# Turning the last stage's weights ahead of time, through DRAM, instead of inside the last stage

## The reference

```
def _L1_ffn_ref(x, gate_wq, gate_scale, up_wq, up_scale, down_wq, down_scale):
    def _dequant_linear(x, wq, scale):
        w = wq.astype(jnp.float32) * scale[:, None]
        return jnp.einsum('bsh,oh->bso', x, w)
    gate = _dequant_linear(x, gate_wq, gate_scale)     # gate_wq, up_wq: 1792 x 512
    up = _dequant_linear(x, up_wq, up_scale)
    h = jax.nn.silu(gate) * up
    return _dequant_linear(h, down_wq, down_scale)     # down_wq: 512 x 1792
...
h = _layernorm(x, axis=-1) * (1 + ca) + sa
x = x + ga * _L1_attn_ref(h, w_q, w_k, w_v, w_o)
h = _layernorm(x, axis=-1) * (1 + cb) + sb
x = x + gb * _L1_ffn_ref(h, gate_wq, gate_scale, up_wq, up_scale, down_wq, down_scale)
```

## Time and profile before

| | us |
|---|---|
| median of the runs | 1921.21 (1914.83 to 1922.13) |
| profiled execution, its own time | 1919.16 |
| its span | 1917.2 |
| PE busy | 1840.1 (96%) |
| PE weight loads busy | 1532.2 (80%) |
| DVE busy | 1265.4 (66%) |
| ACT busy | 1108.3 (58%) |
| POOL busy | 473.6 (25%) |
| HBM | 182.04 MB read, 109.05 MB written |

### The profile page before, as it was taken

One profiled execution on the slowest core, in us unless ns is written; L12 is line 12 of the kernel. 1 busy time (PEld: TensorE's weight loads), 2 busy tenths in 40 slices (PEclk: granted clock), 3 DMA queues, 4 the chain that ended last, 5 costly groups with the idle time before them and its releaser, 6 DMA issues. The chain is left out here.

```text
span 1917.2 us, 30131 instructions
## 1 busy us (share of the span) xinstructions
PE 1840.1 (96%) x9099; PEld 1532.2 (80%) x9099; DVE 1265.4 (66%) x3000; ACT 1108.3 (58%) x2581; POOL 473.6 (25%) x472
## 2 busy tenths in 40 slices
PE   6888889999999999999999999999999989999999
PEld 4456668888888888888888888888888867888887
DVE  5588867667677767666666766677676676544534
ACT  5564656667566656666666666666566654433423
POOL 3123242323424131232423123131312131010010
PEclk8898999999999999999999999999999999999999
DMA  9101365565655656576755646556564575111010
GB/s 355 70 1 66 121 193 174 183 211 158 207 175 180 191 157 184 147 226 202 220 173 160 191 141 187 164 163 186 155 186 145 155 236 166 61 50 66 5 60 22
DMA packets 193420, 292.09 MB, mean 152 GB/s; under 512 B 21304, under 2 KB 130872, under 8 KB 193344
## 3 DMA queue, kind: packets, MB, share of 16 engines
q1 hardware_dynamic: 192816, 290.11, 49.6%
q10 hardware_dynamic: 528, 1.05, 0.2%
HBM read 182.04 MB, written 109.05 MB: 152 GB/s over the span
## 5 line engine op out<-in xcount | busy, mean ns | idle before, releaser
L1777 PE MATMUL ps<-hA,wq 128*128 128x512 f32 x1536 | 387.2, 401 | 4.2 <-DVE qT L2253 4.2
L1843 PE MATMUL ps<-wo,oT 128*128 128x512 f32 x1536 | 367.7, 390 | 3.6 <-issue 2.1
L2096 ACT ACTIVATE pt<-pd 128x1280 fp32r<-128x1280 f32 x128 | 163.2, 1275 | 348.6 <-PE ps L1825 308.8
L2278 DVE CUSTOM_DVE_ANT_0 ps<-ps,mask 128x512 f32<-128x512 f32 (+3 forms) x512 | 235.9, 523 | 192.0 <-PE ps L1810 191.8
L1843 PEld LDWEIGHTS ps<-wo,oT 128*128 128x128 f32 x1536 | 287.6, 188 | 65.2 <-issue 5.1
L1777 PEld LDWEIGHTS ps<-hA,wq 128*128 128x128 f32 x1536 | 279.8, 189 | 61.2 <-issue 4.7
L2077 ACT ACTIVATE probs<-ps,nmax 128x512 f32<-128x512 f32 (+3 forms) x512 | 262.7, 532 | 96.5 <-DVE nmax L2278 96.3
L1825 PE MATMUL ps<-pt,V 128*128 128x512 f32 (+2 forms) x1152 | 255.5, 351 | 19.8 <-DVE pt L2302 19.4
L2085 ACT ACTIVATE probs<-probs,rinv 128x512 f32<-128x512 f32 (+3 forms) x512 | 246.3, 552 | 40.6 <-DVE rinv L2284 40.6
L1825 PEld LDWEIGHTS ps<-pt,V 128*128 128x128 f32 x1152 | 198.2, 192 | 49.0 <-issue 23.5
L1810 PE MATMUL ps<-kT,qT 128*128 128x512 f32 (+2 forms) x1152 | 225.3, 340 | 0.0
(11 more groups left out here) (236 smaller groups left out, 2612.9 us busy)
## 6 DMA issues: line engine op xcount, KB each, us to landing
turned_blocks<-tp SPq DMA_DIRECT2D x128, 640.0 KB, 3.0
pd<-turned_blocks SPq DMA_DIRECT2D x512, 160.0 KB, 3.3
wq_next<-in_L_attn_w_q_dram SPq DMA_DIRECT2D x16, 1024.0 KB, 7.0
wo_in<-in_L_attn_w_o_dram SPq DMA_DIRECT2D x16, 1024.0 KB, 7.2
wm<-in_L_wmod_dram SPq DMA_DIRECT2D x6, 2048.0 KB, 13.4
turned_values<-tv SPq DMA_DIRECT2D x32, 256.0 KB, 3.6
X<-in_L_attn_x_dram SPq DMA_DIRECT2D x4, 1024.0 KB, 11.1
wk_in<-in_L_attn_w_k_dram SPq DMA_DIRECT2D x16, 256.0 KB, 3.2
```

The source lines that it names most:

```text
L1777: last = nc.tensor.matmul(ps[:, bank, :], w[i][:, c, cols], hT[k][:, c, b * S:(b + 1) * S], start=(c == 0 and n == 0), stop=(c == DC - 1 a ...
L1843: last = nc.tensor.matmul(ps[:, bank, :], oT[x_][:, b, h, r * P:(r + 1) * P], wo[y_][:, h, :], start=(h == 0 and n == 0), stop=(h == GQ - ...
L2096: nc.scalar.activation(flat(pt[0][:]), flat(pd[:, u % 2]), ACT.Copy).then_inc(phi_done, 1)
L2278: nc.vector.tensor_tensor_reduce(out=v, in0=v, in1=mask[:, TB * P - KEYS[i]:], scale=-1.0, scalar=3e38, op0=ALU.add, op1=ALU.min, accum_ou ...
```

## The change

The 42 tiles of weights are cast and turned in attention's second half, groups 8 to 14, six tiles a group (two values of j), in units 1, 2, 3, 5, 6 and 7. For a tile, SP loads the int32 weights into `xr` one unit ahead (`load_tile`), ACT casts them to float in place, DVE turns the 32 x 32 blocks from `xr` into `hf_chunk` (`turn_tile`: two instructions of 256 columns for gate and up, one of 512 for down), and SP stores the four quadrants of partitions into a new DRAM tensor `turned_weights` (`store_tile`, four DMAs). Gate and up tiles are written in runs of 64 elements (256 B), down tiles in runs of 128 (512 B). `xr` and `hf_chunk` served the chunks of the second pair in groups 1 to 4 and are free later.

In the last stage the weights of a step j, gate, up and down together (768 KB), come back by four DMAs straight into the place where they are kept (`load_turned`). From j = 4 on a load waits for the gate product of step j - 4. The casts, PE's transposes, DVE's copies, the tensor `wb` and the identity in bf16 are gone. The elements of a kept gate or up tile lie in another order now, so PE reads the 128 columns of a block with a step of two elements (`weight`), and a down tile as runs of 32 elements (`down_weight`).

```diff
-                return [sb(late, f"gw{j}", [P, DC, P], F32R), sb(late, f"uw{j}", [P, DC, P], F32R),
-                        sb(late, f"dw{j}", [P, D], F32R)]
+                return sb(late, f"w{j}", [P, 3, D], F32R)
...
-                    body(NKV, False)
+                    body(NKV, False, True)
                     with eng.Fori(NKV + 1, NG - 1) as g:
-                        body(g, False)
+                        body(g, False, True)
...
+                TILE_UNITS = (1, 2, 3, 5, 6, 7)
+                turned_w = nc.dram_tensor("turned_weights", [FC, QD, 3, NQD, D], F32, kind="Internal").ap()
+                turned_v = turned_w.rearrange("(m e) j k b (a x) -> e k a m j b x", e=2, a=NQD)
+                turned_halves = turned_w.rearrange("(m e) j k b (h a x) -> e k a m j (b h) x", e=2, h=2, a=NQD)
...
+                def weight(j, k, c):
+                    return kept_weight(j, k).rearrange("p (h f e) -> p h e f", h=2, e=2)[:, c // 2, c % 2]
+
+                def down_weight(j):
+                    return kept_weight(j, 2).rearrange("p (a o i) -> p o a i", a=NQD, o=DC)
...
+                        def store_tile(g, i):
+                            m, e, k = steps_of(g), i % 2, i // 2
+                            sp.wait_ge(s["w_turned"], tile_no(g, i))
+                            for a_ in range(NQD):
+                                src = hf_chunk[QD * a_:QD * (a_ + 1), :]
...
+                                sp.dma_start(dst, src).then_inc(s["w_kept"], 16)
+
+                        def load_turned(j):
+                            if j >= 4:
+
+                                sp.wait_ge(s["gate"], j - 3)
+                            for b_ in range(NQD):
+                                rows_ = slice(QD * b_, QD * (b_ + 1))
+                                if j < FC - 1:
+                                    sp.dma_start(ww[j][rows_].bitcast(F32), turned_w[j, :, :, b_]).then_inc(ld_w[j % 4], 16)
...
+                                if keeps:
+                                    if u in TILE_UNITS:
+                                        store_tile(g, TILE_UNITS.index(u))
+                                    if u + 1 in TILE_UNITS:
+                                        load_tile(g, TILE_UNITS.index(u + 1))
+                                if not more and u == 6:
+                                    load_turned(1)
+                                if not more and u == 7:
+                                    load_turned(2)
+                                    load_turned(3)
+
+                                    sp.wait_ge(wo_split, GQ * NG)
+                                    load_turned(0)
...
                             if first:
-                                pe.wait_ge(s["prepped"], 3 * j + 3)
+                                pe.wait_ge(*loads_of(j))
...
-                            if j + AHEAD < FC:
-                                for q in range(3 * (j + AHEAD), 3 * (j + AHEAD) + 3):
-                                    turn_weights(q)
...
+                                if keeps and u in TILE_UNITS:
+                                    act.wait_ge(ld_w[0], 16 * tile_no(g, TILE_UNITS.index(u)))
+                                    nc.scalar.activation(xr[:], xr[:].bitcast(I32), ACT.Copy).then_inc(s["w_cast"], 1)
...
+                                if keeps and u in TILE_UNITS:
+                                    turn_tile(g, TILE_UNITS.index(u))
...
+                        def turn_tile(g, i):
+
+                            dve.wait_ge(s["w_cast"], tile_no(g, i))
+                            if not (at_group(g, NKV) and i == 0):
+                                dve.sem_inc(waits_seen, 1)
+                                dve.wait_ge(s["w_kept"], 16 * NQD * (tile_no(g, i) - 1))
+                            if i // 2 < 2:
+                                for h in range(2):
+                                    last = nc.vector.transpose(
+                                        out=hf_chunk[:].rearrange("p (b h i e) -> p h e b i", b=NQD, h=2, e=2)[:, h],
+                                        in_=xr[:, 2 * h:2 * h + 2, :].rearrange("p c (b j) -> p c b j", b=NQD))
```

More of the change, by code:

```diff
@@ L1507, in body @@
                                     sp.dma_start(at_first[:], att_t[0]).then_inc(ld_at_first, 16)
-                                if not more and u >= 6:
-                                    for q in range(2 * (u - 6), 2 * (u - 6) + 2):
-                                        load_weights(sp.dma_start, q)
                                 reached(sp, o_full, UNITS * g + (u - 1))
@@ L1953, in down @@
                                 for k in range(2):
-                                    last = nc.tensor.matmul(ps[:, t, :], hd[j][k][:, t * P:(t + 1) * P], ww[j][2][:],
+                                    last = nc.tensor.matmul(out, hd[j][k][:, t * P:(t + 1) * P], down_weight(j),
                                                             start=(j == 0 and k == 0), stop=(j == FC - 1 and k == 1))
```

224 lines of the change are left out of this document (82 added, 142 removed).

## The result

| | before | after |
|---|---|---|
| median, measured side by side | 1914.11 us (1911.41 to 1922.77, 20 runs) | 1920.33 us (1913.07 to 1932.79, 20 runs) |
| profiled execution, its span | 1917.2 | 1922.9 |

The ratio is 1.0033, 95% interval 1.0017 to 1.0049: the changed kernel is slower by 6.2 us, with 3.3 to 9.4 inside the interval. Forecast was 1909.

What follows compares the result with a forecast made beforehand. TensorE (PE) was taken as the bound, busy for all 530 us of attention's second half. 1919.2 - 16 (last stage) + 5 (attention) = 1908.2, or 1910.2 from the median of the runs shown; stated as 1909, range 1902 to 1914.

Steps and rivals of the forecast that it cites:

- Two access patterns change: Last stage: reading down weights in runs of 32 and gate and up weights with step two costs 0.
- The outer bound, +134: Last stage, strided gate and up loads: at twice 188 ns, each of 896 matmuls takes 376 instead of 226.
- Group 8, taken at 3 with bounds 1 to 8: Attention group at 885 to 970 us: its queue is already full, so the tiles cost PE 3 us.
- The last stage, -16, bounds 14 to 17.5: Last stage: removing transposes and casts saves 10.6 + 2.0 + 1.7 + 1.1 + 0.9 = 16.3 us, taken as 16.
- I cost the loads at 0: Last stage: 14 loads of 768 KB arrive in time; first weights there near 1568, first pair about 1573; cost 0.
- a wait of PE for it as a sign of being wrong: First batch of the last stage: PE waiting on the turned weights would show the prediction wrong.
- Groups 9 to 14, taken at 0.3 each: Attention, unit 6 to 7: tile lands late, PE waits 0.3 us per group; six groups 2 us, bounds 0 and 18.
- A: Attention's queue is tighter: packets near 83 ns, 3.0 us in six groups and 8 in the first, +26, 1929; chance 0.21.
- B: DMA engines bound the seven attention groups: 2001 at 165 ns a packet, 1935 to 1940 at about 120; chance 0.14.
- C: Last stage: the strided weight load costs from 227 ns on; twice 188 gives 2042; chance 0.06.
- D: Gain eaten in the flush: only the nine even sets of transposes count, 9 us, giving 1915; chance 0.04.
- The chance of 0.55: Whole kernel: probability given to the forecast, range 1902 to 1914, and to faster by about 0.5%, 9.6 us.

Runs made afterwards that it cites:

- e1_contig: Changed kernel with int32 tile rows loaded in another order and stepped DVE transposes, so TensorE reads all kept weights contiguously: 1916.73 us, ratio to before 1.0000.
- e3_psum_runs: Changed kernel with gate, up and down weights read contiguously and the down product written into PSUM in runs of 32: 1915.37 us, ratio to before 0.9994.

## Why the prediction failed, step by step

With three traces of each, the changed part adds up to: the last stage's gain, 178.2 - 165.4 = 12.8 up to the first down product; group 8, +8.7; the pace behind the first down product, +7.4; group 9, +0.1. Net +3.4. Forecast was -11, and the 14.4 between them are: the reads 8.9 (taken at 0), group 8 5.7 (8.7 for 3), the last stage 1.7 (14.3 for 16, at the old pace of the pairs), less 1.9 in the other groups (0.1 for 2). The ratio says +6.2, with 3.3 at its lower end; the 2.8 between are not traced to a row, and lie within what the stretch ahead of group 8 moves by.

- **"Two access patterns change", both taken at 0: this is the step that failed.** Measured 7.4 + 14 pairs x 0.11 = 8.9 us (9.1 by e1_contig against the changed kernel). The argument was that up to 226 ns of load nothing shows. The load record did stay under that, at 193 ns, and the matmuls came 233 apart all the same; with loads of 309 they came 235 apart. The rule compared the wrong two numbers: the pace did not follow the load's length on either side of 226. For the down weights I argued from the outputs product, and read it wrongly: its result is written into PSUM in runs of 32, but its moving operand `pt` is read in runs of 128, 96 or 64 elements. The access patterns in the trace of before say so ([128,4] with a median of 227 ns from matmul to matmul, against [32,4,4] and 233 for the down product after). Only the writing of short runs had been priced, and e3_psum_runs shows that it is indeed free. The outer bound, +134, was so far off that it hid how dear 3% of 1344 matmuls already is.
- The Trainium skill, "SBUF — State Buffer", section "Door 1: The DMA port swizzle", gave 0 for a step of two fp32 elements, since each 16-byte line is hit twice. The runs disagree: 233 ns for 226.6 on the stationary operand, and on the moving operand the same step gives 452, half the pace. The measurement decides.
- **Group 8, taken at 3 with bounds 1 to 8:** 8.7, just outside. The place was right (its full queue), but I priced the queue only through pd. What was missed is what stood behind the tile's stores in SP's order: the output stores, and through POOL's clearing of acc the whole chain to PE. It also fell out of the bounds since behind the wait of 5 us the clock was low (0.50 from 974 to 980 us).
- **The last stage, -16, bounds 14 to 17.5:** within its bounds. 12.8 with the slower pairs in it, 14.3 at the old pace. The turning is gone, and the pair behind the wait for the down gates is no longer slow. Nearly all of it lies behind the first pair (76.4 us from there to the first down product before, 64.2 after, means of three). From group 15's start to the first pair only 0.6 was gained (101.8 to 101.1), where it was to start about 1.3 sooner.
- **"I cost the loads at 0": wrong for the first one.** The prediction named it as the most exposed, with 5 us to spare (there near 1568, used near 1573), and named a wait of PE for it as a sign of being wrong. It took 14.6 us from the first of twelve issues to the landing of the last, 7.6 of issuing (0.64 us an issue where the four pd loads take 0.43 each) and 7.0 from then on, where 10.5 were counted. PE waited 2.07, 0 and 0.82 us for it in the three traces. It is a small part of the miss, up to 2 us. The later loads made PE wait nowhere.
- **Groups 9 to 14, taken at 0.3 each:** 0.0. A packet of 256 B took 20.9 ns where I had taken 40, so a store of 1024 of them 1.3 us of the 16 engines instead of 2.6, nearer to the end at which the prediction left nothing.
- **Rivals.** A (each of six groups loses 3 us) and B (the engines become the bound) did not come: no group but 8 is longer, 256 B stores landed in 2.5 us, and the DMA share was 0.72, not 1. The Trainium skill, "DMA: Bandwidth & Descriptors", table "Specifications", speaks of read-modify-write below 512 B; at 20.9 ns for a packet of 256 B and 33.0 for one of 512 B, so 1.3 times as much for a byte, no large price shows here. In B one number does not follow from its own sum: at 120 ns a packet it gives 2.8 us in each of seven groups, so about 1923 us and not 1935 to 1940. C came in kind, at 5.9 us for the 896 strided loads (9 with the down product's share) instead of 134, and without its threshold at 227 ns. D did not come.
- The chance of 0.55 for faster by over 0.5% leaned on that sum. The rows I had could not price a strided read, and a 3% price on all matmuls of a stage was between two bounds, 0 and +134, of which I took the lower one as if it were near.

## What to carry to other kernels

An access pattern on an operand of TensorE is paid on every matmul: multiply the smallest change by the count before calling it free, and move the permutation to where it is free (here PSUM's side of the product, or the rows that a load puts on each partition). When work is moved under other work, one stage of the loop is usually not like the others: look in it for what else the same queue carries and who stands behind that, and leave that stage out. When a load must be there in time, count the issuing of everything that stands ahead of it in its queue and not only its bytes. Six tiles a group were free and seven were not, so a result of "no cost at all" says nothing on how near the edge is.

## What the runs showed of the hardware that I had not expected

- A weight load with a step of four fp32 elements lasts 309 ns instead of 188, but the matmuls come only 235 ns apart for 227.
- A moving operand with a step of two takes 452 ns for 512 columns, one with a step of four 463, one in runs of 8 only 231.
- A moving operand in runs of 128 elements is read at the plain pace (227 ns, outputs product before), one in runs of 32 at 233; writing PSUM in runs of 32 makes no difference (e3_psum_runs, 6.35 us for 28 matmuls).
- A DVE transpose of 128x512 that writes with a step of four elements: 1131 ns for 712. With a step of two, 128x256 took 421 for 401.
- DMA writes of 256 B: 20.9 ns of engine time for each packet, against 33.0 for one of 512 B (mean of reads and writes); a store of 1024 of them landed 2.5 us after issue.
- Issuing a load of 192 KB from `turned_weights` took SP 0.64 us (twelve in 7.62 us), issuing a pd load 0.43 us (four in 1.73 us).
